# Attention kernel: q and k rows stored part by part and read by 64-partition transfers, with projections at other slots

## What is computed

```python
x = x + 0.5 * ffn(layernorm(x))            # ffn: real(ifft(fft(x) @ w)) + bias
left = layernorm(x)[..., :128]
q, k, v = left @ Wq.T, left @ Wk.T, left @ Wv.T       # 16 heads of 8
att = softmax(einsum('nqhd,nkhd->nqkh', q, k) / 4, axis=2)
x = x + einsum('nqkh,nkhd->nqhd', att, v).reshape(N, S, 128) @ Wo.T + bo
x = x + 0.5 * ffn(layernorm(x))
```

## Time and profile before

| | us |
|---|---|
| median of 3 runs | 323.85 (323.42 to 325.58) |
| the profiled execution's own time | 321.85 |
| its span in the trace | 320.0 |
| PE matmul busy | 298.6 (93%) |
| ACT busy | 259.0 (81%) |
| DVE busy | 190.1 (59%) |
| POOL busy | 97.6 (31%) |
| DMA, mean of the 16 engines, queue of SP | 54.0% |

### The profile page before, as it was taken

How to read it: one execution, slowest core, us unless ns; L and a number is a source line. 1 busy time by engine, 2 the same in 40 slices (tenths; PEclk the granted TensorE clock), 3 DMA queues, 4 the chain that set the end, 5 groups by cost and what they waited for, 6 DMA issues and landing times.

```text
span 320.0 us, 8915 instructions
## 1 busy us (share of the span) xinstructions
PE 298.6 (93%) x3449; PEld 113.9 (36%) x3449; DVE 190.1 (59%) x550; ACT 259.0 (81%) x287; POOL 97.6 (31%) x112
## 2 busy tenths in 40 slices
PE   8898898879999999899999999899999999898995
PEld 5644333133332433343333433343333323232333
DVE  0687538446775677566775778458755623360254
ACT  2214988978898989988999889798999999899921
POOL 6734701312514045043604152313600340034004
PEclk9999999999999999999999999999999999999999
DMA  7835369718565757749555847658464475212102
GB/s 202 311 133 173 94 217 165 211 71 132 198 216 155 184 114 265 214 145 169 200 192 170 153 114 270 200 153 146 132 182 153 123 152 171 87 65 68 36 33 68
DMA packets 29892, 49.87 MB, mean 156 GB/s; under 512 B 3600, under 2 KB 16272, under 8 KB 28944
## 3 DMA queue, kind: packets, MB, share of 16 engines
q1 hardware_dynamic: 29152, 48.79, 54.0%
q10 hardware_dynamic: 688, 0.40, 0.7%
HBM read 31.34 MB, written 17.83 MB: 154 GB/s over the span
## 4 chain that ended last, share of the span: by engine, by line
PE 61%; DMA 12%; DVE 8%; SPq 8%; issue 6%; ACT 4%; POOL 1%; PEldq 0%; DVEq 0%; ACTq 0%
PE misc L718 22%; PE ot L826 21%; PE scores L798 11%; SPq L400 7%; DMA q_scr<-qp 5%; DMA QS<-q_scr 4%; ACT probs L668 4%; DMA leftT<-left_scr 3%; PE scores L685 2%; PE scores L718 1%; PE scores L692 1%; DVE left_blocks L966 1%; DVE lh L957 1%; DVE stats L939 1%; POOL rstd L548 1%
## 5 line engine op out<-in xcount | busy, mean ns | idle before, releaser
L668 ACT ACTIVATE probs<-scores 128x1024 f32<-128x1024 f32 x256 | 244.0, 1030 | 26.8 <-PE scores L798 23.9
L826 PE MATMUL ot<-probs,VS 128*32 128x512 f32 x1024 | 134.1, 594 | 4.8 <-ACT probs L668 3.4
L798 PE MATMUL scores<-QS,KS 32*128 32x512 f32 x512 | 64.8, 495 | 3.8 <-DMA QS<-q_scr 2.4
L798 PEld LDWEIGHTS scores<-QS,KS 32*128 32x128 f32 x512 | 24.5, 181 | 111.1 <-ACT probs L668 100.5
L826 PEld LDWEIGHTS ot<-probs,VS 128*32 128x32 f32 x1024 | 30.7, 109 | 28.5 <-ACT probs L668 7.6
L561 POOL TENSOR_TENSOR x_out<-x,half_bias 128x512 f32<-128x512 f32 x7 | 9.0, 1288 | 98.1 <-DVE x L1012 98.1
L1017 DVE SCALAR_TENSOR_TENSOR x_out<-misc,rstd,x_out 128x256 f32<-128x256 f32 x28 | 13.5, 484 | 37.7 <-PE misc L718 32.7
L546 POOL TENSOR_SCALAR veps<-mv 128x4 f32<-128x4 f32 (+1 forms) x25 | 5.7, 228 | 92.1 <-DVE mv L946 92.1
L718 PE MATMUL misc<-half_ffn,xT 128*32 128x256 f32 x448 | 32.1, 386 | 0.0
L718 PE MATMUL misc<-half_ffn,xT_in 128*32 128x256 f32 x400 | 27.7, 385 | 1.8 <-DVE half_ffn L1188 1.3
L548 POOL TENSOR_TENSOR rstd<-veps,power 128x4 f32<-128x4 f32 (+1 forms) x25 | 25.2, 1008 | 2.1
(11 more groups left out here) (126 smaller groups left out, 265.9 us busy)
## 6 DMA issues: line engine op xcount, KB each, us to landing
KS<-k_scr SPq DMA_DIRECT2D x56, 128.0 KB, 4.7
QS<-q_scr SPq DMA_DIRECT2D x56, 128.0 KB, 3.1
x_in<-x SPq DMA_DIRECT2D x8, 512.0 KB, 5.4
xT_in<-x_t SPq DMA_DIRECT2D x8, 512.0 KB, 6.8
k_scr<-kp SPq DMA_DIRECT2D x8, 512.0 KB, 2.8
q_scr<-qp SPq DMA_DIRECT2D x8, 512.0 KB, 4.3
x_scr<-x_blocks SPq DMA_DIRECT2D x7, 512.0 KB, 3.7
xT<-x_scr SPq DMA_DIRECT2D x7, 512.0 KB, 4.7
```

What stands on the lines that cost most here:

```text
L668: nc.scalar.activation(probs[u % PRING][:, :, :], scores[u % SRING][:, :, :], ACT.Exp, scale=SCORE_SCALE).then_inc(exp_done, 1)
L798: last = mm(scores[(u + j // 2) % SRING][:, j % 2, :], KS[b % 2][rows, slot, kt * P:(kt + 1) * P].bitcast(F32R), QS[b % 2][rows, slot, :]. ...
L826: last = mm(ot[COL * j:COL * (j + 1), :], VS[b % 2][:, kt, h, :], probs[(u + j // 2) % PRING][:, j % 2, :], start=s % 8 == 0, stop=s % 8 == 7)
```

## The change

q_scr and k_scr get the same layout: part, then row (lane and feature, 32 of them), then slot, then tokens. With it a part of all lanes is one transfer: k_rows and q_rows write 64 partitions, every second one, from rows of 8 KB, two transfers for K and two for Q. For q, each DRAM row is read for two partitions. The store of k now writes two 2 KB pieces for each partition, as q's did. Weights' rows, head_ones and pick follow the layout; their sizes are the same. leftT gets a second buffer.

The tables change: KT for the next batch in slots 0 and 1 in place of V; V in slot 9; F2 one to two slots later; nothing of KT in 14 and 15. In BEGIN, QT follows KT in slot 3 and the F1 halves are spread over slots 4 to 8, V over 9 and 10; the KT jobs in slot 15 go. In LATE, KT is in 0 and 1, QT in 5 and 6, V in 7 and 8. The square of k moves to quad 4, that of q in batch 0 to quad 7 and in batch 6 to quad 8. left_half and turn_left of batch 0 move from slots 7 and 8 to 10 and 11. SP's order is written anew.

```diff
SLOTS = H // LANES
-ROW_SIGNALS = 16 * 2 * PARTS * LANES
+ROW_SIGNALS = 16 * 2 * PARTS
...
-STEADY = {0: [("V_0", 1, RIGHT), ("F1_0a", 2, LEFT)], 1: [("F1_0", 2, LEFT), ("V_1", 1, RIGHT)],
+STEADY = {0: [("KT_0", 1, RIGHT), ("F1_0a", 2, LEFT)], 1: [("F1_0", 2, LEFT), ("KT_1", 1, RIGHT)],
-          9: [("F2_0a", -1, LEFT), ("F2_0", -1, LEFT)], 10: [("N", 1, RIGHT), ("F2_1a", -1, LEFT)],
-          13: [("F2_3a", -1, LEFT), ("F2_3", -1, LEFT)], 14: [("KT_0", 2, RIGHT)], 15: [("KT_1", 2, RIGHT)]}
+          9: [("V_0", 1, RIGHT), ("V_1", 1, LEFT)], 10: [("N", 1, RIGHT), ("F2_0a", -1, LEFT)], 11: [("F2_0", -1, LEFT)],
...
-BEGIN = {1: [("LT", 1, LEFT)], 2: [("KT_0", 1, LEFT), ("KT_1", 1, RIGHT)],
+BEGIN = {1: [("LT", 1, LEFT)], 2: [("KT_0", 1, LEFT), ("KT_1", 1, RIGHT)], 3: [("QT_0", 1, LEFT), ("QT_1", 1, RIGHT)],
...
 
-    q_scr = nc.dram_tensor("q_scr", [PARTS, Dh, H, S], F32, kind="Internal").ap()
-    k_scr = nc.dram_tensor("k_scr", [H, Dh, PARTS, S], F32, kind="Internal").ap()
+    q_scr = nc.dram_tensor("q_scr", [PARTS, LANES * Dh, SLOTS, S], F32, kind="Internal").ap()
+    k_scr = nc.dram_tensor("k_scr", [PARTS, LANES * Dh, SLOTS, S], F32, kind="Internal").ap()
 
 
...
         xT = sb("xT", [P, C, P // 32, T, 32])
-        leftT = sb("leftT", [P, S])
+        leftT = [sb(f"leftT{i}", [P, S]) for i in range(2)]
         left_blocks = sb("left_blocks", [P, HD // 32, T, 32])
         x2_blocks = sb("x2_blocks", [P, E // 32, T, 32])
...
         def store_k(eng):
-            eng.dma_start(k_scr.rearrange("h d j s -> (h d) j s"), kp[:, :, :]).then_inc(k_stored, 16)
+            eng.dma_start(k_scr.rearrange("j r h s -> (r h) j s"), kp[:, :, :]).then_inc(k_stored, 16)
 
         def store_q(eng):
-            eng.dma_start(q_scr.rearrange("i d h s -> (d h) i s"), qp[:, :, :]).then_inc(q_stored, 16)
-
-        def k_rows(eng, par, slots, lane, loaded):
-            heads = slice(SLOTS * lane + slots.start, SLOTS * lane + slots.stop)
-            for i in range(PARTS):
-                first = ROWS * lane + PARTS * Dh * i
-                eng.dma_start(KS[par][first:first + PARTS * Dh, slots, :],
-                              k_scr[heads].rearrange("h d j s -> (d j) h s")).then_inc(loaded, 16)
-
-        def q_rows(eng, par, slots, lane, loaded):
-            heads = slice(SLOTS * lane + slots.start, SLOTS * lane + slots.stop)
-            for j in range(PARTS):
-                first = ROWS * lane + j
-                eng.dma_start(QS[par][first:ROWS * (lane + 1):PARTS, slots, :],
-                              q_scr[:, :, heads, :].rearrange("i d h s -> (i d) h s")).then_inc(loaded, 16)
+            eng.dma_start(q_scr.rearrange("i r h s -> (r h) i s"), qp[:, :, :]).then_inc(q_stored, 16)
+
+        def k_rows(eng, par, slots, i, loaded):
+
+            eng.dma_start(KS[par][i::PARTS, slots, :],
+                          k_scr[:, :, slots, :].rearrange("j r h s -> r j h s")).then_inc(loaded, 16)
+
+        def q_rows(eng, par, slots, i, loaded):
+            eng.dma_start(QS[par][i::PARTS, slots, :],
+                          q_scr[i][:, slots, :].unsqueeze(1).to_broadcast([LANES * Dh, PARTS, slots.stop - slots.start, S])).then_inc(loaded, 16)
 
 
         @block.sync
...
                 wait(sp, rows_loaded, ROW_SIGNALS * (b - 1))
                 store_k(sp)
 
-            def k_in(b, lanes):
+            def k_in(b, part=slice(None)):
                 wait(sp, quad_done, QUADS * (b - 1))
                 sp.wait_ge(k_stored, 16 * (b + 1))
-                for lane in lanes:
-                    k_rows(sp, b % 2, slice(0, SLOTS), lane, rows_loaded)
+                for n in range(PARTS)[part]:
+                    k_rows(sp, b % 2, slice(0, SLOTS), n, rows_loaded)
 
             def q_out(b):
                 sp.wait_ge(evacuated, last_count("QT", b))
                 store_q(sp)
 
-            def q_in(b, lanes):
+            def q_in(b, part=slice(None)):
                 sp.wait_ge(q_stored, 16 * (b + 1))
-                for lane in lanes:
-                    q_rows(sp, b % 2, slice(0, SLOTS), lane, rows_loaded)
+                for n in range(PARTS)[part]:
+                    q_rows(sp, b % 2, slice(0, SLOTS), n, rows_loaded)
 
             def x2_through(b):
                 sp.wait_ge(x2_turned, b + 1)
...
             def leftT_in(b):
-                for kind in ("V", "QT"):
-                    sp.wait_ge(evacuated, last_count(kind, b - 1))
+                for kind in ("KT", "QT") if b == 2 else ("KT", "QT", "V"):
+                    sp.wait_ge(evacuated, last_count(kind, b - 2))
+                if b == 2:
+                    sp.wait_ge(first_v_ready, 1)
                 sp.wait_ge(left_stored, 16 * (b - 1))
-                sp.dma_start(leftT[:, :].rearrange("p (g s) -> p g s", g=P // 32),
+                sp.dma_start(leftT[b % 2][:, :].rearrange("p (g s) -> p g s", g=P // 32),
                              left_scr.rearrange("g f k s -> (f k) g s")).then_inc(left_loaded, 16)
 
...
 
-            for it in range(B):
-                if it == 0:
-                    load_x(3)
-                    k_out(1)
+            load_x(3)
+            k_out(1)
+            q_out(1)
+            k_in(1)
+            q_in(1)
+            left_through(2)
+            leftT_in(2)
+            for it in range(1, B):
+                if it + 3 < B:
+                    load_x(it + 3)
+                if it >= 2:
+                    store_out(it - 2, 1)
                 if it + 1 < B:
-
-                    k_in(it + 1, range(0, LANES // 2 if it == B - 2 else LANES))
-                if it >= 1:
-                    x2_through(it - 1)
-                    xT_in_from(it - 1)
-                if it == B - 2:
-                    k_in(it + 1, range(LANES // 2, LANES))
-                if it >= 1 and it + 3 < B:
-                    load_x(it + 3)
+                    k_out(it + 1)
+                    k_in(it + 1, slice(0, 1))
+                x2_through(it - 1)
+                if it + 1 < B:
+                    k_in(it + 1, slice(1, None))
+                xT_in_from(it - 1)
                 if it + 1 < B:
                     q_out(it + 1)
                 if it + 2 < B:
                     left_through(it + 2)
                 if it + 1 < B:
-                    q_in(it + 1, range(0, 2))
+                    q_in(it + 1, slice(0, 1))
                 if it + 2 < B:
                     leftT_in(it + 2)
                 if it + 1 < B:
-                    q_in(it + 1, range(2, LANES))
-                if it >= 1:
-                    store_out(it - 1, 0)
-                if it + 2 < B:
-                    k_out(it + 2)
-                if it >= 1:
-                    store_out(it - 1, 1)
+                    q_in(it + 1, slice(1, None))
+                store_out(it - 1, 0)
+            store_out(B - 2, 1)
             store_last_out(B - 1)
             sp.wait_ge(out_stored, 32 * (B - 1) + 16 * T)
 
...
-                    if s == (2 * 2 if it else 2 * 5):
+                    if s == (2 * 4 if it else 2 * 5):
                         square(kp, sq_k, kp_step, it + 1)
-                    if s == (2 * 10 if it else 2 * 9):
+                    if s == (2 * (8 if it == B - 2 else 10) if it else 2 * 7):
                         square(qp, sq_q, qp_step, it + 1)
                 act.wait_ge(scores_ready, u // 2 + 1)
...
-                        if s == (8 if it else 7):
+                        if s == (8 if it else 10):
                             left_half(it + 2, range(0, 2))
-                        if s == (9 if it else 8):
+                        if s == (9 if it else 11):
                             left_half(it + 2, range(2, T))
                             turn_left(it + 2)
...
         heads[SLOTS * lane + slot] = h
-    by_head = (heads[:, None] * Dh + np.arange(Dh)[None, :]).ravel()
-    by_dim = (heads[None, :] * Dh + np.arange(Dh)[:, None]).ravel()
+    by_row = (heads.reshape(LANES, 1, SLOTS) * Dh + np.arange(Dh)[None, :, None]).ravel()
     head_ones = np.zeros((P, 2, 32), np.float32)
-    head_ones[np.arange(P), 0, np.arange(P) // Dh] = 1.0
-    head_ones[np.arange(P), 1, np.arange(P) % H] = 1.0
+    head_ones[np.arange(P), :, SLOTS * (np.arange(P) // ROWS) + np.arange(P) % SLOTS] = 1.0
 
     x_t = np.asarray(L0_attn_x).reshape(B, P, T, E).transpose(0, 3, 2, 1).reshape(B, E, S)
...
-                        row = ROWS * lane + PARTS * Dh * i + PARTS * d + j
-                        pick[(SLOTS * lane + slot) * Dh + d, 0, slot, j, row] = 1.0
-                        pick[d * H + SLOTS * lane + slot, 1, slot, i, row] = 1.0
+                        row = ROWS * lane + TERMS * d + PARTS * j + i
+                        pick[ROWS * lane + SLOTS * d + slot, 0, slot, j, row] = 1.0
+                        pick[ROWS * lane + SLOTS * d + slot, 1, slot, i, row] = 1.0
 
     cos_var = np.cos(angle).astype(np.float32)
```

(9 more changed lines are left out.)

27 lines of the change are left out of this document (13 added, 14 removed).

## The result

| | before | changed |
|---|---|---|
| median, us | 323.63 (322.07 to 325.58, 4 runs) | 318.75 (317.01 to 320.35, 4 runs) |
| ratio | | 0.9868, 95% interval 0.9826 to 0.9909 |
| profiled execution, us | 321.85 | 320.35 |
| its span, us | 320.0 | 318.5 |

The change makes the kernel 1.3% faster, 318.75 us where 318.3 was forecast. The profile shows that the agreement of forecast and median covers an error and is in part luck. The profiled execution was the slowest of four; the spans of the others were 315.2, 316.7 and 317.2 us. The forecast of the span was 314.4, so even the fastest of them is 0.8 us above it.

A forecast was written before the change was run, and what follows sets the result against it. The exponentials on ACT set the pace, with PE bound in double slots and late q rows and leftT at boundaries. Gains of 2.1, 3.0 and 0.5 us took the span from 320.0 to 314.4, the time to 318.3, range 315.5 to 323.0.

The forecast's parts named there:

- (c): Batch 0: fewer double slots and no wait for q rows at its end; 35.5 to 33.4 us, gain 2.1 us.
- (b): Batches 1 to 5: leftT double-buffered, V and K's projection moved; steady batch 34.5 us, sum 173.5 against 176.46, gain 3.0.
- (d): Batch 6: single jobs, early q rows and K's square beside a double take 0.5 us off 31.82; other parts 0.
- (a): Row transfers: last q row lands 7 us after q's store, boundary just covered; 0.5 us of stalls in all.
- (e): The x loads on SP move behind the q rows; no loss counted.
- from span to median: Forecast span 314.4 us plus 1.85 around it plus 2.0 from profiled execution to median made 318.3 us.
- rival 1: Slower: 64-partition pairs move at K's pace, q rows stall five boundaries, about 11 us together; 329 us, chance 0.12.
- rival 3: More gain: no bank hold in slot 1 and rows at about 5 us; 316.0 us, chance 0.13.
- the batches at 34.3 to 34.9 us: Sign that the forecast is right: batches 1 to 5 each take this long.
- the boundary quads under 2.0: Sign that the forecast is right: last quads before the next batch take 1.8 to 2.0 us.
- QS landing over 8.4 us: Sign that the forecast is wrong: q's rows land later than this after q's store, the point where scores stall.
- The ports: Row transfer rate: trace leaned towards the 16-port rule; the other formula's 4.4 us for the q pair was set aside.

The follow-up runs named there:

- e6: Changed kernel with all q rows issued behind leftT's store but ahead of leftT's load; 315.57 us in the first set, 314.52 us in the second.
- e1: Changed kernel with both q row transfers issued ahead of leftT's store and load; 314.77 us, and 315.36 us when run again.
- r0: Changed kernel run again with no edit, as reference for the follow-up runs; 318.34 us, ratio 0.989 to the kernel before.
- e2: Changed kernel with the x loads moved behind the output store on SP's queue; 317.18 us, ratio 0.986 to the kernel before.
- e9: Changed kernel with e6's order and also e2's move of the x loads behind the output store; 314.73 us.
- e4: Changed kernel's tables, two leftT buffers and SP order, but the DRAM layouts and 16-partition transfers of the kernel before; 322.62 us, ratio 1.002.
- e5: Kernel before with only the new layouts and 64-partition transfers; tables, one leftT and SP order as before; 316.91 us, ratio 0.985.

## Why the prediction was right or wrong

**Right, batch 0, (c).** 33.2 us against 33.4. Both holds of the bank are there and each makes a quad of 2.86 us, and q's square cost nothing beyond its slot.

**Right, the steady batch, (b).** Without stalls it is 34.43 us (e6) where 34.5 was said. The hold by slot 1 is there, in the quad that it delays: quad 3 is 2.47 us in batches 1 to 5 of every run with these tables, against 2.30 for a plain double. It costs 0.17 of the 0.2 estimated. leftT is off the chain as forecast: the kernel before waited 2.7 us for it in 3 places, the changed one nowhere. V's pair in slot 9 costs nothing on PE. It does cost on DVE, which was not in my sum: the V copies come ahead of the left half, whose store is issued some 0.6 us later in batches 3 to 5 (in batch 3, 25.6 against 24.95), and this chain set when q's second half was issued.

**Right, batch 6, (d).** 31.3 us, as forecast. And batch 2's leftT, for which (b) took 0.5 us, landed at 65.2 us, 0.4 us before its job: 0.

**Wrong, the last q row, (a).** "So the boundary is just covered, with 0.4 to 1 us to spare" was the step that failed. I took 7 us from q stored to the last landing. In the two profiled executions of the changed kernel it was 9.4 and 9.8 in batch 3, the latter with q stored at 160.1 and the last row at 169.9. The 9.8 consist of 1.9 us until the second half is issued, which waits on SP for the store of the left half, and 8.0 us until it lands. I had counted leftT's load between the halves but not that wait, and I had read the landing from the x pair, which ran beside less. That the order is the cause is shown by e1, beside r0 (314.77 against 318.34 us, ranges apart), and again by e6: in both the last row lands 5.2 to 8.4 us from q stored and no boundary stalls. How the excess divides between the wait, the company and the instruction packets is open. The point from which scores stall, 33.5 us into the batch, was right within 0.3 us: at 32.9 (e6), 31.5 (e1) and 33.4 us (e2) batch 3 has no stall, at 35.4 (r0) and 36.0 it stalls by 1.6 and 2.2.

**Wrong, the x loads, (e).** "They are queued behind these, so I count no loss" does not hold. They are issued from 1.8 us behind the second half on, while its rows are still under way. Without them behind it the second half lands in 5.4 to 5.7 us in batches 1 to 3 (e2) and not in 5.7 to 8.0. But batches 4 and 5, which load no x, stall by 2.5 and 0.8 us in the two profiles, so x is not the whole; and with q's rows issued together (e6 against e9) it costs nothing. (a) and (e) together are the 0.5 us of the sum that measured 3.4 and 5.8.

**Right by a wrong part: from span to median.** I added 2.0 us because the median of before was 2.0 above its profiled execution. In the changed kernel the profiled execution was 1.6 above the median. The span forecast was 1 to 4 us too low and the 2 us made up for most of it. Had I summed to 317, the value that the spans have at the median, the same addition would have given 321. So the closeness of 318.3 to 318.75 is luck, and the two us are no fixed overhead. Landings that differ from one execution to the next are a likely part of them: e6, with no stall, has 314.06 to 315.87 in its second set, the kernel before 319.8 to 330.9 over 18 runs. Not all of it is landings: of these 18, six at a granted clock of 0.995 took 323.7 to 324.9, and the one of 330.9 had 0.989. And e6's first set went up to 317.31. The parts were not separated.

**The rivals.** The mechanism of rival 1, rows that land beyond 8.4 us from q's store, is what took place (8.4 to 10.5 us in the slower profile), with another cause: not K's pace for 64 partitions but the queue and what runs beside. Its price, 11 us, was twice to three times too high. Rows at 5 us, the condition of rival 3, are nearly what e1 has (5.5). Of the signs that I named, the batches at 34.3 to 34.9 us and the boundary quads under 2.0 failed, and that of QS landing over 8.4 us came true. I had the parts' weights wrong as well: I gave the transfers almost no gain of their own (a saved wait, at most) and the tables all of it. e4 and e5, each beside the kernel before, show the reverse.

**The ports.** An estimate by the fit of the Trainium skill ("SBUF — State Buffer", section "The DMA setup-cost knee"), taken for the pair's megabyte as one transfer, is 4.4 us. With nothing in front, in e1, the pair lands 3.9 and 4.9 us after issue, 0.6 apart, so 5.5 from the first issue; in the changed kernel up to 9.8. The measurement decides. The Trainium skill's rule ("SBUF — State Buffer", section "Door 1: The DMA port swizzle") that the rate goes with the ports reached, 4 of 16 for 16 adjacent partitions, agrees in direction with K: 9 us before, 5.4 in e5. But e5 also makes a piece 8 KB in place of 2 and two issues (1.17 us) of eight (3.60 us), and these were not tried apart. My reading that K's megabyte in 6 us "fits the slow end" was loose: it is 175 GB/s, where four ports of 27.2 GB/s make 109. I was wrong to lean on the 7.3 us of the x pair for the pair alone; for the pair in company even that was short.

One transfer of all 128 partitions for K or for Q was not tried.

## What to carry to other kernels

Where one queue issues everything, the latest transfer of a chain is set by the waits in front of it. Look at what each in-order wait keeps back, and issue the transfers that the next stage needs before those with slack; here this was worth some 3.5 us, and the new slots of the jobs none without it and the wide transfers. Do not count transfers that are "queued behind" a late one as free without a row that shows it. Time a part of a change both ways, alone and left out, before its gain is put down to the whole: here the transfers alone gave what the whole change gave, and what the new tables add was never seen by itself.

## What the runs showed of the hardware

In the ten profiles with wide transfers, q's store of 512 KB, issued in batches 1 to 6, took between 2.8 and 5.6 us. In batches 1 to 5 it mostly has no other transfer of the program beside it. What goes with the long ones there is one packet of the instruction queue. Two stretches of the changed kernel, the store of batch 3 and that of batch 1:

```profile
q1 hardware_dynamic: 273, 0.53, 27.2%
q8 instruction: 1, 0.02, 2.1%
...
q_scr<-qp SPq DMA_DIRECT2D x1, 512.0 KB, 4.8
```
```profile
q1 hardware_dynamic: 272, 0.52, 44.7%
...
q_scr<-qp SPq DMA_DIRECT2D x1, 512.0 KB, 2.9
```

The first has 4.8 us and a 16 KB instruction packet of 1.7 us; the second has 2.9 and no such packet. Over the ten profiles, a packet counts if it is under way at some time between 0.9 us after the store's issue and 0.9 before its landing. Of the 50 stores of batches 1 to 5, the 19 without one took 2.8 to 3.4 us. The 13 whose packet began at most 0.5 us after their issue took 3.2 to 3.6. The 18 whose packet began later, 1.0 to 2.2 us after it, took 4.3 to 5.3. (Batch 6's stores took 4.3 to 5.6 us with a packet or without, beside other transfers, and say nothing of it.)

The records of single packets say more. The store is 256 packets of 2 KB, so a sixteenth of it is 16. In the slow store of batch 3 all but 16 of them have ended 2.4 us after the issue; in the quick one all have at 2.5. The instruction packet ends at 2.66 us, and the 16 follow it, the last 13 of them back to back at 0.084 us each, up to 4.32 us. In 17 of the 18 slow stores the landing comes 2.1 us behind the end of the instruction packet (2.0 in the other), wherever that end lies, from 2.3 to 3.2 us after the issue. The trace doesn't name the engine of a packet, but by these numbers one sixteenth of the store, one engine's share, stands behind the instruction packet and sets the landing.

The program meets the packet at about the same place in each execution: the stores issued in batches 3 and 4 took 4.3 us or more in every kernel with wide transfers and the new tables. In e5, with the old tables, it falls elsewhere, and these two took 2.9 and 3.2 us. A kernel made to move the packet alone was not tried.
